# Row maxima of a head group taken by halves of the queries, and attention begun behind the first half, in a causal-attention and expert-FFN kernel

## The reference, cut to what matters

```python
cq = _gelu(x @ wq + bq)                     # queries and keys come out of projections,
q = _gelu(concat([q_c, q_r])).reshape(b, s, H, HD).transpose(0, 2, 1, 3)   # rotation, gelu
scores = einsum('bhqd,bhkd->bhqk', q, k) / sqrt(HD)
scores = where(causal, -inf, scores)
attn = softmax(scores, axis=-1)             # the maximum of each row is taken off inside
out = einsum('bhqk,bhkd->bhqd', attn, v)
# then: @ wo + bo, layernorm, residual; then a top-2 of 8 experts FFN on 4096 rows, layernorm
```

## Time and profile before

| | µs |
|---|---|
| median of 3 runs | 827.97 |
| the profiled execution, its own time | 826.73 |
| its span in the trace | 825.00 |
| stage one's compute (L590 to L602) ends on PE | 66.5 |
| DVE's last addition of stage one (L554) ends | 67.3 |
| POOL's last low part of stage one (L430) ends | 72.3 |
| PE's first maxima matmul | 73.7 |
| PE, behind the barrier (L308), begins | 93.9 |
| first exponential of group 0 | 104.2 |
| last exponential of group 15 | 628.0 |
| PE busy | 735.9 (89%) |
| DVE busy | 619.7 (75%) |
| ACT busy | 516.9 (63%) |
| POOL busy | 335.2 (41%) |

### The profile page before, as it was taken

How to read it: one execution, slowest core, us unless ns; L and a number is a source line. 1 busy time by engine, 2 the same in 40 slices (tenths; PEclk the granted TensorE clock), 3 DMA queues, 4 the chain that set the end, 5 groups by cost and what they waited for, 6 DMA issues and landing times.

```text
span 825.0 us, 17277 instructions
## 1 busy us (share of the span) xinstructions
PE 735.9 (89%) x5620; PEld 352.9 (43%) x5620; DVE 619.7 (75%) x1956; ACT 516.9 (63%) x1063; POOL 335.2 (41%) x518
## 2 busy tenths in 40 slices
PE   5885699999999999999999989999989979898983
PEld 2431133333334334334333433433435768686772
DVE  5995888988886896887888697789454756565885
ACT  4883056666766777667687666677888634343563
POOL 3773122222221332224543225354246277464672
PEclk9996579999999999999999999999999999999997
DMA  4689171431632414405245143251321425235413
GB/s 130 181 215 210 39 171 27 68 54 17 114 59 48 69 50 83 76 14 97 50 87 81 40 68 67 58 97 34 91 73 37 107 73 164 73 88 167 124 68 118
DMA packets 78386, 71.81 MB, mean 87 GB/s; under 512 B 27138, under 2 KB 58275, under 8 KB 78115
## 3 DMA queue, kind: packets, MB, share of 16 engines
q1 hardware_dynamic: 69672, 59.84, 32.8%
q0 software_dynamic: 4352, 8.99, 3.5%
q10 hardware_dynamic: 4274, 1.87, 0.9%
HBM read 44.24 MB, written 23.94 MB: 83 GB/s over the span
## 4 chain that ended last, share of the span: by engine, by line
PE 58%; DVE 12%; issue 7%; ACT 7%; DMA 2%; POOL 1%; SPq 0%; DVEq 0%; ACTq 0%; POOLq 0%
PE ps L2272 15%; PE ps L2299 14%; PE ps L279 11%; DVE x_in L290 5%; ACT expT L2006 4%; PE ps L1779 4%; PE ps L1760 2%; PE ps L1762 2%; PE ps L1761 2%; PE ps L1768 2%; PE ps L2249 1%; ACT rows L749 1%; PE ps L1686 1%; DMA expT<-expert_rows 1%; PE ps L974 1%
## 5 line engine op out<-in xcount | busy, mean ns | idle before, releaser
L2006 ACT ACTIVATE expT<-ps 128x512 f32<-128x512 f32 (+1 forms) x640 | 333.1, 554 | 148.6 <-PE ps L2299 141.5
L290 DVE CUSTOM_DVE_ANT_0 x_in<-ps,mask 128x1024 bf16<-128x1024 f32 (+7 forms) x512 | 364.3, 754 | 64.4 <-PE ps L279 60.8
L2299 PE MATMUL ps<-q_space,k_space 96*128 96x512 bf16 (+3 forms) x768 | 223.6, 334 | 8.7 <-ACT expT L2006 5.1
L279 PE MATMUL ps<-k_space,q_space 96*128 96x512 bf16 (+3 forms) x768 | 197.4, 343 | 24.6 <-DVE mx L290 15.2
L2272 PE MATMUL ps<-expT,vr 128*9 128x256 f32 (+1 forms) x2560 | 178.4, 360 | 0.9 <-POOL expT L1960 0.9
L1960 POOL TENSOR_SCALAR_AFFINE_SELECT expT<-expT 128x512 f32<-128x512 f32 x128 | 79.8, 635 | 195.2 <-ACT expT L2006 194.7
L2299 PEld LDWEIGHTS ps<-q_space,k_space 96*128 96x128 bf16 x768 | 62.1, 98 | 160.2 <-ACT expT L2006 104.0
L279 PEld LDWEIGHTS ps<-k_space,q_space 96*128 96x128 bf16 x768 | 64.2, 100 | 88.4 <-DVE mx L290 48.4
L1302 POOL DMA_INDIRECT expert_rows<-expT,tile_to x72 | 70.6, 980 | 43.4 <-ACT expT L1384 22.5
L739 POOL DMA_INDIRECT sorted_rows<-rows,places x64 | 64.1, 1001 | 58.9 <-ACT expT L2006 33.9
L2272 PEld LDWEIGHTS ps<-expT,vr 128*9 128x9 f32 x2560 | 41.4, 88 | 92.2 <-issue 47.6
(11 more groups left out here) (243 smaller groups left out, 910.7 us busy)
## 6 DMA issues: line engine op xcount, KB each, us to landing
q_space<-q_parts SPq DMA_DIRECT2D x48, 192.0 KB
expT<-sorted_rows SPq DMA_DIRECT2D x72, 65.0 KB, 2.2
k_space<-k_parts SPq DMA_DIRECT2D x32, 128.0 KB
q_parts<-parts SPq DMA_DIRECT2D x24, 128.0 KB, 2.8
k_parts<-parts SPq DMA_DIRECT2D x24, 128.0 KB, 2.8
k_space<-k_parts SPq DMA_DIRECT2D x16, 192.0 KB
expT<-expert_rows SPq DMA_DIRECT2D x10, 256.0 KB, 3.4
v_ones<-v_st SPq DMA_DIRECT2D x8, 288.0 KB, 4.3
```

The lines of the kernel that those rows point to most:

```text
L279: last = nc.tensor.matmul(psw[:, at + lo:at + hi], qr[:, g % RING, hh, qi * P:(qi + 1) * P], kr[:, g % RING, hh, lo:hi], start=True, stop= ...
L290: last = nc.vector.tensor_tensor_reduce(out=unread[:, odd, col:col + width], in0=psw[:, 2 * CT * odd + col:2 * CT * odd + col + width], in ...
L2006: act.activation(expT[:, (NS * g + s) % PTN, hh, 0:width], ps[:, B_S + hh % 2, 0:width], ACT.Exp, scale=SCALE).then_inc(exp_ok, 1)
L2299: last = nc.tensor.matmul(ps[:, B_S + hh % 2, col:col + m], kr[:, g % RING, hh, kt * P:(kt + 1) * P], qr[:, g % RING, hh, q0:q0 + m], star ...
```

## The change

What it does:

- An item's tiles are now grouped by halves of the queries: items 0 to 7 (`FIRST_ITEMS`, two a head) cover queries 0 to 511 of all four heads, items 8 to 23 (`SECOND_ITEMS`, four a head) queries 512 to 1023. The two halves of the negation follow the same cut. `q_space` is laid out by halves (`qv`), so each query load is two DMAs (13 DMAs a group instead of 10) and each half of the negated maxima is one DMA instead of two.
- Slots 0 to 11 need only the first half of the negated maxima; PE waits for the second at slot 12 (`s in (0, HALF0)`).
- Stage one ends with 16 of group 0's items (0 to 15) and the first neg; POOL splits and ACT (not SP) places it there. ACT also zeroes two PSUM banks there, in place of DVE's memset behind the barrier. Group 0's items 16 to 23 stand two to a slot in slots 0 to 3 of group 0, and its second neg at slot 6. The new planner gives each item a cost (6 for a first-half item, 8 for a second-half item or "out", 2 for a neg) and lays all 24 items of group g+1 in group g; the second neg of group g stands at slot 5 of group g itself, the first neg of group g+1 at slot 20.
- POOL's `split_neg` of the second half stands ahead of step 0 of its own group (step 1 for group 0), behind `side` of step 9 of the group before.
- SP in stage one: group 0's pieces stand ahead of the stores of chunks 3, 4 and 5 (its waits on the constant rows too), and the last chunk's store ahead of group 1's load. In the attention stage SP loads group g+2 at slot 8.

```diff
 
-HEAD_ITEMS = [[(7, 0)], [(3, 0), (0, CT)], [(6, 0)], [(2, 0), (1, CT)], [(5, 0)], [(4, 0)]]
-MAX_ITEMS = [(hh, tiles) for hh in range(GH) for tiles in HEAD_ITEMS]
+FIRST_ITEMS = [[(3, 0), (0, CT)], [(2, 0), (1, CT)]]
-IN_ONE = 18
+NM0 = GH * len(FIRST_ITEMS)
+OWN_FROM = NM0 + 8
 
 
 def wide_items(g):
 
-
+    def maxima_of(off, a, b):
+        return [("max", off, i) for i in range(a, b)]
 
     if g == -1:
-        seq = [("max", 1, i) for i in range(NM)]
-        return [seq[:IN_ONE + 1] + [("neg", 1, 0)] + seq[IN_ONE + 1:] + [("neg", 1, 1)]]
-    nxt = [("max", 1, i) for i in range(0 if g == 0 else EARLY, NM)] if g + 1 < G else []
-    neg = [("neg", 1, 0), ("neg", 1, 1)] if g + 1 < G else []
-    early = [("max", 2, i) for i in range(EARLY)] if g + 2 < G else []
-    prev = [("out", -1, 1)] if g > 0 else []
+        return [maxima_of(1, 0, NM0 + 2) + [("neg", 1, 0)] + maxima_of(1, NM0 + 2, OWN_FROM)]
+    more = g + 1 < G
+    slots = [[] for _ in range(GH * NS)]
     if g == 0:
-        seq = nxt[:17] + neg[:1] + nxt[17:22] + [("out", 0, 0)] + nxt[22:] + early[:4] + neg[1:] + early[4:]
+        for i, item in enumerate(maxima_of(0, OWN_FROM, NM)):
+            slots[i // 2].append(item)
+        begin, lead = (NM - OWN_FROM) // 2, 2
     else:
-        seq = nxt[:11] + prev + neg[:1] + nxt[11:] + early[:1] + [("out", 0, 0)] + early[1:4] + neg[1:] + early[4:]
-    slots, at = [[] for _ in range(GH * NS)], 0
-    for i, item in enumerate(seq):
-        at = max(at, i * (GH * NS - 1) // max(N_ITEMS, len(seq)))
+        begin, lead = 0, 4
+    seq = maxima_of(1, 0, lead if more else 0) + [("neg", 0, 1)] + maxima_of(1, lead, NM0 + 4 if more else lead)
+    seq += [("out", -1, 1)] if g > 0 else []
+    seq += (maxima_of(1, NM0 + 4, NM0 + 6) + [("neg", 1, 0)] + maxima_of(1, NM0 + 6, NM0 + 10)) if more else []
+    seq += [("out", 0, 0)] + (maxima_of(1, NM0 + 10, NM) if more else [])
+    costs = [{"max": 6 if which < NM0 else 8, "neg": 2, "out": 8}[kind] for kind, _, which in seq]
+    total, at, sofar = max(sum(costs), 200), begin, 0
+    for item, cost in zip(seq, costs):
+        at = max(at, begin + sofar * (GH * NS - 1 - begin) // total)
         if item[0] == "out":
             at = max(at, GH * (LAG + 2 + (0 if item[2] else HALF0 - 1)))
+        if item[:2] == ("neg", 0):
+            at = max(at, begin + 5 if begin == 0 else begin + 2)
         slots[at].append(item)
+        sofar += cost
     return slots
...
+        qv = qr.rearrange("p r h s -> p r (h s)").rearrange("p r (f h t) -> p r f h t", f=2, h=GH)
...
+        IN_DMAS = 13
...
+                if i == 4:
+                    sp.dma_start(vr[:, r], vd[b][:, :, hg * GH * VW:(hg + 1) * GH * VW]).then_inc(group_in[r], DMA)
+                    continue
                 row, end = 3 * HD * i, 3 * HD * (i + 1)
-                sp.dma_start(qr[row:end, r], qg).then_inc(group_in[r], DMA)
+                for f in range(2):
+                    sp.dma_start(qv[row:end, r, f], qg[:, :, CT * f:CT * (f + 1)]).then_inc(group_in[r], DMA)
...
+        def split_neg(pool, g, f):
+
+            pool.wait_ge(wide_used, used_after("max", g, (NM0, NM)[f] - 1))
+            base = 10 * g + 5 * f
+            n = [negs[:, g % 2, f, s] for s in range(3)]
+            m = mx[:, g % 2].rearrange("p (h q) -> p h q", q=QT)[:, :, QT // 2 * f:QT // 2 * (f + 1)]
...
+        def turn_neg(pe, odd, g, f):
+            pe.wait_ge(split, 10 * g + 5 * (f + 1))
+            nc.tensor.transpose(psw[0:3 * GH * QT // 2, 2 * CT * odd:2 * CT * odd + P // 2].bitcast(BF16),
+                                negs[:, g % 2, f].rearrange("p s h q -> p (s h q)"), identb[:]).then_inc(wide_ready, 1)
+
+        def keep_neg(dve, n, odd, g, f):
+            dve.wait_ge(wide_ready, n + 1)
+            if g > 0:
+                dve.wait_ge(neg_in[(g - 1) % RING][f], DMA * ((g - 1) // RING + 1))
+            nc.vector.tensor_copy(negT[:, f, :], psw[0:3 * GH * QT // 2, 2 * CT * odd:2 * CT * odd + P // 2]
+                                  .bitcast(BF16)).then_inc(wide_used, 1)
+
+        def place_neg(eng, g, f):
+            eng.wait_ge(wide_used, used_after("neg", g, f))
+            eng.dma_start(qv[ROWS:MROWS, g % RING, f].rearrange("p h t -> p (h t)"), negT[:, f, :]).then_inc(neg_in[g % RING][f], DMA)
...
                 for c in range(1, CHUNKS):
+                    if c == GROUP0_AT:
+                        sp.wait_ge(rows_in, DMA * 2 * RING)
+                        for i in range(2):
+                            sp.wait_ge(stored[i], DMA * NSTORE)
+                    if 0 <= c - GROUP0_AT < 3:
+                        load_group(sp, 0, ([4, 0], [1], [2])[c - GROUP0_AT])
                     store((c - 1) // 2, (c - 1) % 2)
+                    if c == 1:
+                        load_group(sp, 0, [3])
                     if c in FILL_AT:
                         r = FILL_AT.index(c)
                         fill_rows(sp, kr, r, ROWS, KROWS, 1).then_inc(rows_in, DMA)
                         fill_rows(sp, qr, r, MROWS, KROWS, 0).then_inc(rows_in, DMA)
-                    if c == GROUP0_AT:
-                        sp.wait_ge(rows_in, DMA * 2 * RING)
-                        for i in range(2):
-                            sp.wait_ge(stored[i], DMA * NSTORE)
-                    if c >= GROUP0_AT:
-                        load_group(sp, 0, [c - GROUP0_AT])
+                store(PAIRS - 1, 1)
                 load_group(sp, 1)
-                store(PAIRS - 1, 1)
                 for p in range(2):
                     sp.wait_ge(stored[p], DMA * NSTORE * PAIRS)
...
+                split_neg(pool, 0, 0)
...
+                act.wait_ge(mask_ok, 2)
+                act.wait_ge(v_ready, CHUNKS)
+                for i in range(2):
+                    act.activation(ps[:, B_O + i], mask[:, 0:CT], ACT.Copy).then_inc(zeroed, 1)
+                place_neg(act, 0, 0)
...
-                for k in range(IN_ONE):
-                    wait(pe, wide_used, k - 1)
-                    scores_for_max(pe, k % 2, 0, k)
+                for g, _, kind, of, which, n in WIDE:
+                    if g == -1:
+                        wait(pe, wide_used, n - 1)
+                        if kind == "max":
+                            scores_for_max(pe, n % 2, of, which)
+                        else:
+                            turn_neg(pe, n % 2, of, which)
...
-                def place_neg(g, f):
-                    for h in range(2):
-                        sp.dma_start(qr[ROWS:MROWS, g % RING, 2 * f + h, :],
-                                     negT[3 * QT * h:3 * QT * (h + 1), f, :]).then_inc(neg_in[g % RING][f], DMA)
-
-                for f in range(2):
-                    sp.wait_ge(wide_used, used_after("neg", 0, f))
-                    place_neg(0, f)
...
+                LOAD_AT = GH * LAG
...
                 for g in range(G):
-                    if g + 2 < G:
-                        load(g + 2)
                     items = of_group(g)
                     for slot in range(GH * NS):
+                        if slot == LOAD_AT and g + 2 < G:
+                            load(g + 2)
                         side(g, slot)
                         for p, _, at, kind, gg, which, n in items:
                             if at == slot and kind == "neg":
-                                sp.wait_ge(wide_used, n + 1)
-                                place_neg(gg, which)
+                                place_neg(sp, gg, which)
                 sync_behind(sp)
...
-                for f in range(2):
-                    split_neg(0, f)
                 constants(pool)
...
-
+                        if s == int(g == 0):
+                            split_neg(pool, g, 1)
...
-                        if s in (HALF0, HALF0 + 3) and g + 1 < G:
-                            split_neg(g + 1, int(s > HALF0))
+                        if s == HALF0 + 1 and g + 1 < G:
+                            split_neg(pool, g + 1, 0)
                         side(g, s)
...
-                v.memset(ps[:, B_O:B_O + 2, :], 0.0).then_inc(zeroed, 1)
...
-                for p, e in enumerate(WIDE):
-                    if e[0] == -1 and e[5] >= IN_ONE:
-                        item(p, *e[2:])
...
-                for p, e in enumerate(WIDE):
-                    if e[0] == -1 and e[5] >= IN_ONE:
-                        item(p, *e[2:])
-                pe.wait_ge(zeroed, 1)
+                pe.wait_ge(zeroed, 2)
...
-                            if s == 0 and hh % 2 == 0:
-                                pe.wait_ge(neg_in[g % RING][hh // 2], NEG_DMAS * DMA * (g // RING + 1))
+                            if s in (0, HALF0) and hh == 0:
+                                pe.wait_ge(neg_in[g % RING][s // HALF0], DMA * (g // RING + 1))
...
```

74 lines of the change are left out of this document (30 added, 44 removed).

## The result

The changed kernel takes 839.17 µs (median of 4 runs, 835.6 to 842.38) against 828.93 for the kernel before on the same chip (4 runs, 827.39 to 831.92): ratio 1.0118, 95% interval [1.006, 1.0176]. It is slower by over 0.5%; 817.9 was forecast. The profiled execution has a span of 835.1 against 825.0.

The account below looks back on a forecast made before the run. PE was taken as the bound from group 1 on, with a serial prologue ahead of it. Terms -15.0 + 2.2 + 4.2 - 1.5 = -10.1 turned 826.7 into 816.6, the median 827.97 into 817.9; range 809 to 828.

Parts of the forecast that it names:

- Step 1: Stage one: group 0's load issued ahead of chunk 5's stores; PE slips 1.0, maxima begin at 68.3, 5.4 µs earlier.
- the landing of 2.7 and of 2.0: Stage one: DMA landing delays assumed, 2.7 µs for constant rows; chunk 3's stores issued by 52.5, landed by 54.5.
- Step 2: Stage one's maxima: 16 items and the first neg end at 85.5 instead of 93.9, a gain of 8.4 µs.
- Step 3: Behind the barrier: first exponential at 86.8 instead of 104.2, group 1 at 125.4 instead of 140.4, 15.0 µs gained.
- the 0.5 for a rest at half clock: Group 0 behind slot 6: 0.5 µs added to its remaining 34 slots for a rest of time at half clock.
- Step 4: Group 14: eight items moved into it, 24 instead of 16, 2.2 µs lost.
- Step 5: Slot 5, groups 1 to 15: PE waits 0.7 for POOL's split in six groups, 4.2 µs lost; nothing at slot 12.
- Step 6: Item spacing by cost in the groups: 12 items instead of 13 in slots 16 to 37, 1.5 µs gained.
- the late second neg: Rival: second neg's DMA lands too late for slot 12 in every group, 21 µs lost, 839; chance 0.08.
- The prologue only moves: Rival: the eight items cost as much behind the barrier as ahead of it, no change, 828; chance 0.12.
- SP did not hold the barrier: Rival judged: delayed stores make SP's 13 DMAs end at 90 and hold the barrier, 4.5 lost, 822.4; chance 0.15.
- Full clock: Rival: PE's clock stays at 1.00 through the maxima, 1.5 more there and 1.5 in group 0, 815; chance 0.10.

Follow-up runs that it names:

- e6: e5 with the wait for the constant rows made by PE ahead of the first maxima instead of by SP; ratio 0.9966 to the kernel before.
- e1: The kernel before with only the change's SP order in stage one (waits and group 0's loads ahead of stores); ratio 1.0027.
- e9: The changed kernel run again with no edit; ratio 1.0074 to the kernel before.
- e3: The changed kernel with POOL's split of the second neg moved ahead of its side work in the group before; ratio 1.0115 to the kernel before.
- e14: e5 with only the second neg moved to slot 5 of its own group, POOL's split ahead of step 0; ratio 1.0066 to the kernel before.
- e5: The changed kernel keeping its halves, stage one and group 0 start, but with the old plan of items and negs afterwards; ratio 0.997 to the kernel before.
- e4: The changed kernel with planner costs 8 and 7 instead of 6 and 8, spacing items nearly evenly; second neg at slot 6; ratio 1.0036 to the kernel before.
- e8: The kernel before run again with no edit; one execution, 830.44 µs.
- e11: e12 with all 24 of group 0's items in stage one, none in group 0's slots, second split a step earlier; ratio 0.9927 to the kernel before.
- e12: e5 with group 0's load in three pieces behind the stores of chunks 3, 4 and 5; ratio 0.9912 to the kernel before.
- e13: e12 with the first neg's DMA issued by SP ahead of group 1's load instead of by ACT; 822.05 µs, ratio 0.9915 to the kernel before.

## Why the prediction was wrong

The sum said -10.1, the profile says +10.1. The 20.2 lie in these steps.

**Step 1, wrong by 6.4** (74.7 for 68.3). The way of the loss was worked out, from SP's wait through chunk 3's stores to chunk 5's `parts` and chunk 7's turn, and every term in it too small. The last constant row took 4.8 from issue to SP's next, not 2.7. With the load among the stores, chunk 3's last went out at 55.18 and had landed at 59.54, where 54.5 was forecast. PE's slip was priced at 1.0 with a bound of 2.5; its idle stretch was 5.5, and it fell to half clock in it. Of the 5.0 by which chunk 5's `parts` came later than forecast, 3.0 are SP's wait for the rows (49.5 for 46.5), 0.3 the issues and 1.8 the landing (3.75 behind the end of the last issue for 2.0). The term that failed is the landing of 2.7 and of 2.0: it was read where one store was waited for, and laid on DMAs that go out amid others. Nor is SP's wait the root by itself, for without it `parts` came only 0.9 earlier (e6). e1 shows the same stall alone. First maxima stood at 74.0 to 78.2 in the nine executions with the change's order of loads, e6 with them (mean 76.0), at 73.7 and 75.7 in the two of the kernel before, and at 69.1 to 71.5 in the four with the load behind the stores (mean 70.4).

**Step 2, right in the sum, with some luck.** From first maxima to the barrier 17.2 were forecast and 17.2 measured. Two errors cancel: DVE took 6.9 for the eight first-half items where 7.6 was forecast, and PE's turn waited 0.80 for POOL's split, which was counted as covered, so that DVE stood idle 0.79 behind it.

```profile
84.00 0.27 PE L331 MATMUL ps<-identb,negs 128*48 128x128 bf16 x1 [0.80 <-POOL negs L327]
```

The neg's landing was covered as said, but only just: in e9 it is what released PE's first score.

**Step 3, off by 1.5.** The first exponential followed 1.3 behind the barrier as forecast. Group 0 took 40.1 for 38.6. Slot 6 came in time, 10.1 behind the first exponential for 10.7; the rest took 30.0 for 27.9. The term that was too small is the 0.5 for a rest at half clock: it lasted until 110.8, 7.5 behind slot 6.

**Step 4, right.** Group 14 takes 36.18, as group 10 with its 35.9. It grew by 3.9 and group 10, with the same losses of steps 5 and 6, by 1.4: 2.5 for the eight items, where 2.2 was said.

**Step 5, mechanism half right.** PE does wait for POOL at slot 5 in groups behind `root`, 0.58 in group 5; e3 puts it at 2.0 for 4.2. Slot 12 never waits for `negT`'s DMA in groups 1 to 14. What the step missed is the neg as an item among two buffers: e14 shows 6.4 in groups 1 to 13, in which neither POOL's split nor `negT`'s DMA is waited for. The prediction looked at whom the turn waits for, and not at what the maxima lose when the turn takes their buffer where DVE is busiest.

**Step 6, wrong sign.** 1.5 gained was forecast. Over groups 1 to 13 the changed kernel takes 11.4 more than the one before: 1.7 is in e5 already, 6.4 comes with the neg's place, and 3.3 remains for the order and spacing of the items with POOL's part in it. e4 wins 4.6 there by spacing (the neg a slot later with it), so these parts overlap; they don't add up strictly. In the first slots, first-half items come two tiles each, in pieces of 128 to 512 columns, and PE waits for DVE at three of them in group 3 (0.29, 0.30, 0.27):

```profile
201.55 0.45 PE L295 MATMUL ps<-k_space,q_space 96*128 96x512 bf16 x2 [0.29 <-DVE mx L306]
...
204.15 0.45 PE L295 MATMUL ps<-k_space,q_space 96*128 96x384 bf16 x2 [0.30 <-DVE mx L306]
204.97 0.61 PE L295 MATMUL ps<-k_space,q_space 96*128 96x512 bf16 x2 [0.27 <-DVE mx L306]
```

The wrong step is the average: 13 items against 12 over slots 16 to 37 says nothing of the first 12 slots, where the cost ratio 6 to 8 sets the short items closest.

Together: 7.9 to group 1, 10.4 for steps 4 to 6, and 1.9 in group 15 and the last stage, which vary by nearly as much between executions of one kernel (225.0 in the kernel before, 226.7 in e8). The bounds of the single terms, added up, reach 828.9 at the top and not 828; the result lies outside either.

**The rivals.** The time is by chance that of the late second neg (839); that mechanism did not occur. "The prologue only moves" was nearly right for the part it speaks of: e11 and e12 can't be told apart in time. SP did not hold the barrier: its last issue ended at 88.9, DVE's last maximum at 91.5. Full clock came, from 66.5 to 76.7, and fell back in the maxima. The prediction also named its own refutation: "if group 1 begins after 131"; it began at 133.3.

**Left open.** How the 3.3 µs between e14 and the changed kernel divide between the order of the items, their spacing and POOL's split: e3 and e4 changed these in the changed kernel only. And what 24 items would give with e13's neg, which wasn't tried.

## What to carry to other kernels

An item that costs an engine 0.2 µs still takes a buffer. Ask what the engine that empties the buffers is doing at its place, and not only whether its result is early enough. Price a landing by what goes out around it in the changed kernel, and move loads past stores only after asking which compute waits for those stores. A prologue is worth shortening only by what is not then done at the same price behind it; time the same work on both sides of the barrier before counting.
